# A causal attention pass with its score chunks in reverse, and experts whose transposes stand between two products

## The reference

```
att = jnp.einsum('bthd,bThd->bhtT', q, k) / math.sqrt(HD)
att = jnp.where(causal, -jnp.inf, att)
att = jax.nn.softmax(att, axis=-1)
out = jnp.einsum('bhtT,bThd->bthd', att, v).reshape(Bx, Tx, Cx)
...
dispatched = jnp.einsum('sec,sm->ecm', dispatch, tokens)      # 8 experts, capacity 640 slots
h = jax.nn.relu(jnp.einsum('ecm,emf->ecf', dispatched, w1) + b1[:, None, :])   # 128 -> 512
expert_out = jnp.einsum('ecf,efm->ecm', h, w2) + b2[:, None, :]                # 512 -> 128
combined = jnp.einsum('sec,ecm->sm', combine, expert_out)
```

## Time and profile before

| what | value |
|---|---|
| median of 3 runs | 2424.55 us (2423.39 to 2437.38) |
| profiled execution | 2432.8 us |
| its span | 2430.8 us |
| granted clock of PE over it | 0.844 of full speed |
| causal attention of layer 0 | 178 to 549 us of the span |
| scatter of tokens | 664 to 706 us |
| experts | 716 to 821 us |

### The profile page before, as it was taken

The page is one execution under the profiler, slowest core; times in us unless marked ns, Lnnn a source line. Parts: engine busy times, 40 slices in busy tenths (PEclk is TensorE's granted clock), DMA queues, the critical chain, the costliest instruction groups (busy, mean ns, idle before and its releaser), DMA issues. The chain is left out here.

```text
span 2430.8 us, 43279 instructions
## 1 busy us (share of the span) xinstructions
PE 1873.0 (77%) x12804; PEld 976.6 (40%) x12868; DVE 1448.5 (60%) x2514; ACT 1157.3 (48%) x2802; POOL 892.7 (37%) x999
## 2 busy tenths in 40 slices
PE   5528999884618455629999999557999999999996
PEld 3314444432516334422222222234555555555552
DVE  4426767751401233317888888126888888888882
ACT  1115656560003111104667667305777677677672
POOL 3223344341140332310111111116666677666670
PEclk9768889895559765657999989758999999999997
DMA  3432323322013223232333332130111111111110
GB/s 107 133 101 74 112 92 107 108 84 84 14 63 103 83 85 101 72 94 72 99 108 108 104 105 80 65 111 25 31 48 31 33 43 38 39 52 41 38 49 20
DMA packets 137868, 179.90 MB, mean 74 GB/s; under 512 B 14896, under 2 KB 82355, under 8 KB 137520
## 3 DMA queue, kind: packets, MB, share of 16 engines
q1 hardware_dynamic: 135728, 174.59, 23.3%
q0 software_dynamic: 2048, 4.16, 0.6%
HBM read 97.22 MB, written 66.06 MB: 67 GB/s over the span
## 5 line engine op out<-in xcount | busy, mean ns | idle before, releaser
L910 DVE TENSOR_REDUCE M_sb<-banks 128x1 f32<-128x512 f32 (+3 forms) x1024 | 539.8, 581 | 228.0 <-PE banks L727 124.8
L812 ACT ACTIVATE probs_sb<-banks 128x512 f32<-128x512 f32 (+3 forms) x1024 | 473.5, 520 | 254.9 <-PE banks L753 250.8
L724 PE MATMUL banks<-K_sb,Q_sb 72*128 72x512 bf16 (+3 forms) x1024 | 373.8, 371 | 107.8 <-DMA V_sb<-v_dram 71.5
L753 PE MATMUL banks<-Q_sb,K_sb 75*128 75x512 bf16 (+3 forms) x1024 | 358.6, 357 | 5.9 <-ACT probs_sb L812 3.9
L767 PE MATMUL banks<-probs_sb,V_sb 128*32 128x512 f32 (+3 forms) x2048 | 249.9, 556 | 11.8 <-ACT osum_sb L823 8.6
L724 PEld LDWEIGHTS banks<-K_sb,Q_sb 72*128 72x128 bf16 x1024 | 103.2, 101 | 385.2 <-DVE M_sb L910 225.2
L1773 ACT ACTIVATE l_p_sb<-banks,l_nb_sb,l_inv_sb 128x128 f32<-128x128 f32 x512 | 228.0, 465 | 12.7 <-DVE l_nb_sb L1945 12.5
L1851 POOL TENSOR_TENSOR l_inv_sb<-l_clip_sb,l_minus_half_sb 128x16 f32<-128x16 f32 x64 | 186.2, 2909 | 57.2 <-DVE l_clip_sb L1920 55.3
L1859 POOL TENSOR_TENSOR l_pn_sb<-l_p_sb,l_rs_sb 128x512 f32<-128x512 f32 x128 | 150.1, 1173 | 145.5 <-DVE l_rs_sb L1951 144.0
L1844 POOL TENSOR_TENSOR l_ts_sb<-l_t_sb 128x1024 f32<-128x1024 f32 x64 | 153.4, 2396 | 41.1 <-DVE l_t_sb L1899 24.0
L1579 PE MATMUL banks<-lw_sb,l_xs_sb 128*128 128x512 f32 x256 | 127.8, 623 | 26.4 <-DMA l_xs_sb<-hx 22.8
(11 more groups left out here) (205 smaller groups left out, 3575.1 us busy)
## 6 DMA issues: line engine op xcount, KB each, us to landing
Q_sb<-qk_dram SPq DMA_DIRECT2D x192, 96.0 KB
v_dram<-vpad_sb SPq DMA_DIRECT2D x16, 1024.0 KB, 8.5
V_sb<-v_dram SPq DMA_DIRECT2D x64, 256.0 KB
o_dram<-osum_sb SPq DMA_DIRECT2D x64, 256.0 KB, 5.3
l_vs_sb<-l_vt_sb SPq DMA_DIRECT2D x112, 128.0 KB, 2.3
qk_dram<-parts_sb SPq DMA_DIRECT2D x96, 128.0 KB
K_sb<-qk_dram SPq DMA_DIRECT2D x32, 288.0 KB
x_norm_sb<-x SPq DMA_DIRECT2D x24, 256.0 KB, 2.7
```

The lines of the kernel that those rows point to most:

```text
L724: mm = pe.matmul(out[:, 0:width], g.Q[0:RK, slot, h, k * P:(k + 1) * P], g.K[0:RK, slot, hk(h), 0:width], start=True, stop=not causal)
L753: pe.matmul(SB[ring % 3][:, t0:N], g.K[0:RM, q, hk(h), k * P:(k + 1) * P], g.Q[0:RM, q, h, t0:N], start=True, stop=True).then_inc(s["b_sco ...
L812: act.activation(g.probs[:, k, h, t0:N], SB[ring % 3][:, t0:N], ACT.Exp, scale=scale)\
L910: dve.reduce_max(g.M[:, u % 2, k, h:h + 1], SA[ring % 3][:, 0:width], AX.X, negate=True)\
```

## The change

In the causal layer, `a_tile` and `maxima` go through the query chunks from the last to the first (`query_chunk`), 512 keys first and 128 last. `b_tile`, the exponentials and the products with V keep their order. Where the loop index was compared with 0 it is still the loop index.

In `experts`, the transposes of expert e + 1 (`turn`) stand between the first product (`widen`) and the second (`narrow`) of expert e; `exT` and `eh` get two buffers each, and the answer banks alternate across experts. The wait for the biases at an expert's end is gone from PE; the first uses of the second product wait tile by tile. The loads are split: slots have a semaphore of their own and are loaded once the transposes of the expert two before are done; weights and biases are loaded after that expert's answers are stored. The weights of the first two experts are loaded by SP in the block in which GpSimd scatters. The first and last pair are written out ahead of and behind the loop.

```diff
+    def query_chunk(j):
+        return CH - 1 - j if causal else j
...
-            def a_tile(i, u, k, h):
-                n = u * per + k * UH + h
+            def a_tile(i, u, j, h):
+                n, k = u * per + j * UH + h, query_chunk(j)
...
-            def maxima(i, u, k, h):
-                n = u * per + k * UH + h
+            def maxima(i, u, j, h):
+                n, k = u * per + j * UH + h, query_chunk(j)
...
+        @block.sync
+        def _(sp):
+            for e in range(2):
+                load_weights(g, sp, e, e)
...
-    g.eh = g.sb("eh", [P, F // P, CAP])
-    g.exT = g.sb("exT", [P, CAP])
+    g.eh = g.sb("eh", [P, 2, F // P, CAP])
+    g.exT = g.sb("exT", [P, 2, CAP])
...
+                    e = i * 2 + par
+                    if not last:
+                        sp.wait_ge(s["turned"], e + 1)
+                        load_slots(e + 2, par)
+                    sp.wait_ge(s["biased"], (e + 1) * ST)
+                    sp.dma_start(g.answers_by_expert[e], tile(ys[par])).then_inc(s["stored"], 16)
+                    if not last:
+                        load_weights(g, sp, e + 2, par)
...
+            def turn(e, par, nth):
+                pe.wait_ge(g.eload[par], nth * 16 + 16)
+                pe.wait_ge(s["xT"], e * 2)
+                for t in range(ST):
+                    bank, col = (g.bank[0], t * P) if t < 4 else (g.bank[1], 0)
+                    mm = pe.transpose(bank[:, col:col + P], tile(xs[par])[:, t, :], g.ident[:, :])
+                mm.then_inc(s["turned"], 1)
...
+                    widen(e, par, i)
+                    if not (last and par):
+                        turn(e + 1, par ^ 1, i + par)
+                    narrow(e, par)
...
-                    pe.wait_ge(s["biased"], (i * 2 + par + 1) * ST)
...
+                    if not (last and par):
+                        copy_turned(e + 1, par ^ 1)
                     for t in range(ST):
+                        bias(e, par, t)
```

More of the change, by code:

```diff
@@ L1174, in tile, with pairs @@
         return t.rearrange("p a n -> p (a n)")[:, 0:CAP].rearrange("p (s c) -> p s c", c=C)
+    def pairs(engine, two):
+        two(0, True, False)
+        with engine.Fori(1, E // 2 - 1) as i:
+            two(i, False, False)
+        two(E // 2 - 1, False, True)
     with nc.Block() as block:
@@ L1178, in _, with load_slots, two @@
         def _(sp):
[L1179 to L1184, removed]
+            def load_slots(e, par):
                 sp.dma_start(tile(xs[par]), g.slots_by_expert[e]).then_inc(g.eload[par], 16)
-            def two(i, last):
+            def two(i, first, last):
                 for par in range(2):
[L1189 to L1200, removed]
+                    e = i * 2 + par
[6 more added lines that the diff above has]
+                        load_weights(g, sp, e + 2, par)
+            for e in range(2):
+                load_slots(e, e)
+            pairs(sp, two)
             sp.wait_ge(s["stored"], 16 * E)
@@ new lines, in widen @@
+            def widen(e, par, nth):
+                pe.wait_ge(g.ewload[par], nth * 64 + 64)
+                pe.wait_ge(s["xT"], e * 2 + 2)
+                for f in range(FT):
+                    for half in range(2):
+                        n = f * 2 + half
+                        if not (isinstance(e, int) and e * 8 + n < 4):
+                            pe.wait_ge(s["relu"], e * 8 + n - 3)
+                        pe.matmul(g.bank[2 + n % 4][:, 0:HALF], g.ew1[:, par, f * P:(f + 1) * P],
+                                  g.exT[:, par, half * HALF:(half + 1) * HALF], start=True, stop=True)\
+                          .then_inc(s["hidden"], 1)
@@ new lines, in narrow @@
+            def narrow(e, par):
+                pe.wait_ge(s["relu"], e * 8 + 8)
+                for t in range(ST):
+                    if not (isinstance(e, int) and e * ST + t < 2):
+                        pe.wait_ge(s["biased"], e * ST + t - 1)
+                    bank = g.bank[6 + (par * ST + t) % 2]
+                    for f in range(FT):
+                        mm = pe.matmul(bank[:, 0:C], g.eh[:, par, f, t * P:(t + 1) * P],
+                                       g.ew2[:, par, f * C:(f + 1) * C], start=(f == 0), stop=(f == FT - 1))
+                    mm.then_inc(s["answer"], 1)
@@ new lines, in two, with _ @@
+            def two(i, first, last):
+                for par in range(2):
+                    e = i * 2 + par
+                    widen(e, par, i)
+                    if not (last and par):
+                        turn(e + 1, par ^ 1, i + par)
+                    narrow(e, par)
+            turn(0, 0, 0)
+            pairs(pe, two)
+        @block.scalar
+        def _(act):
+            def two(i, first, last):
+                for par in range(2):
+                    e = i * 2 + par
+                    if not first:
+                        act.wait_ge(s["answer"], (e - 1) * ST)
+                    for f in range(FT):
@@ L1232, in _ @@
[L1232 to L1242 removed]
+                            act.wait_ge(s["hidden"], e * 8 + n + 1)
@@ L1253, in _ @@
                     for t in range(ST):
-                        dve.wait_ge(s["answer"], (i * 2 + par) * ST + t + 1)
-                        dve.tensor_tensor(tile(ys[par])[:, t, :], g.bank[6 + t % 2][:, 0:C], g.eb2[:, par, :],
-                                          ALU.add).then_inc(s["biased"], 1)
+                        bias(e, par, t)
+            copy_turned(0, 0)
+            pairs(dve, two)
 def combine(g, x1, x2):
```

70 lines of the change are left out of this document (28 added, 42 removed).

## The result

The changed kernel took 2402.01 us in the median of 4 runs (2399.23 to 2405.19). The kernel before stood at 2430.97 (4 runs, 2423.39 to 2441.49) with the runs made beside it, so its first three runs had come out low. The ratio is 0.9874, 95% interval 0.9838 to 0.9911: about 29 us, or 1.3%, less.

A forecast was written before the change was run, and what follows sets the result against it. PE was taken as the bound, ending last in both touched stages, so its waits were what could change. -2 - 21.1 - 2.3 = -25.4 us from a median of 2424.55 gave 2400 us, range 2388 to 2413.

The forecast's parts named there:

- sum of 25.4 us: Whole kernel: 2 us less in the causal pass, 21.1 in the experts, 2.3 at the experts' start.
- Steady unit: Causal pass: reversed chunks make a unit 9.29 us against 9.52, in 23 units 5.3 us less.
- mask's chain: Causal pass: chunk 3's product waits for GpSimd's mask, 3.13 us after chunk 2's start; chunks 2 and 3 together 3.70 us.
- Unit with the reciprocals: Causal pass, q = 1 in seven batches, waiting on a DMA: +0.5 us each, +3.5 in all, bounds -3.5 and +7.
- arithmetic of the wait: Causal unit q = 1: first reciprocal starts 4.2 us into the unit against 3.30; 0.9 later, minus 0.7, is +0.2.
- rival (the clock): Causal pass: mask's chain out of the way or clock no longer falling in q = 1; -12 us, so 2389; chance 0.13.
- Experts: Experts' stage: a step takes 9.76 us, seven steps 69.3 with branches against 90.42, so 21.1 us less.
- slow first products: Experts: two of seven first products take 6.26 us instead of 4.57; counted as gone, 3.3 us; if they stay, gain 17.8.
- Start: Start of the experts: slots issued first land 2.0 to 3.0 us earlier; 2.3 us less was taken.
- upper end of 3.0: Start of the experts: if descriptors start in order within one queue, slots wait today for four weight transfers; gain 3.0 us.
- Loads: Experts: moved weight loads take about 5.9 us, PE needs them 9.76 later; slack 3.9 us, nobody waits.
- rule of the Trainium skill: Causal pass: frequent micro-idles of PE make the clock oscillate, so 0.2 us waits in every chunk would cost clock; set aside.

The follow-up runs named there:

- the longer chain: The changed kernel with one more small GpSimd operation of 0.19 us ahead of every mask; chunk 3 took 1.82 us against 1.67, the one run 2403.9 us.

## Why the prediction was right, point by point

- *The time.* 2400 was forecast and 2402.0 measured, and that close a hit is luck. The sum of 25.4 us was 3.6 too small against the 29.0 of the runs made side by side, and the starting point of 2424.55 was 6.4 too low, since the first three runs of the kernel before lay below its later medians; the two misses have opposite signs. By stages, in the profiles: causal pass 2 forecast and 5.2 found, seven steps of the experts 21.1 and 22.5, start 2.3 and 1.2.
- *Steady unit.* The steps were 2.44, 3.15, 2.00, 1.70, the profile has 2.44, 3.11, 2.02, 1.67 or 1.68. The unit gained 0.27, not 0.23; the ones with the output projection gained 0.16 (10.28 to 10.12), and the first of the pass 1.1. In 23 units that is about 6 us. That the mask's chain sets chunk 3 was argued from one row and is shown by the longer chain: +0.15 there and nowhere else.
- *Unit with the reciprocals.* +0.5 was taken; over six units the mean went from 15.08 to 15.11, and with the experts' part alone, in the old order too, it is 15.74: by these the sign is open. The arithmetic of the wait was right (reciprocal 4.3 us into the unit, 4.2 forecast).
- *What was missed.* The step that the next unit would stay as it is. It has the output projection, and in the old order the slow clock sometimes lasts into it. The forecast saw one length of slow stretch, the 6.2 us of the earlier trace rows, while the same trace held a batch of 47.9 us beside five of 44.1 to 44.9 and a last one of 38.8. The reversal alone measured -8.7 by medians, not -2; that is the size at which its rival (the clock) had been put, -12, with a chance of 0.13. But the rival's own account, that the clock no longer falls in q = 1, is not what happened: in the changed kernel's profile it still fell once in each of the seven batches, and only the longest stretches are missing. Shown is that stretches of 17 us occur in the old order (four in two profiles) and not in the new one (none in six), and that nothing of the kind is left where the wait is gone. Why a slow stretch lasts 7 or 17 us is not settled.
- *Experts.* Seven steps: 69.3 forecast, 67.9 measured. The loops' branches cost nothing visible, which is most of the 1.4. That the slow first products would go with the waits was right in every profile that has the change. The reason given was too simple: the first product at 771.97 stands behind the same two waits, 0.97 and 1.07 us, and was not slow. The gain from the place of the transposes was measured by itself: 13.3 us in the profile, 14.2 in the time.
- *Start.* 2.3 forecast, 2.4 in the profile, but the first product was slow throughout (7.45 against 6.23), which took back 1.2: the step that an earlier start is kept in full was wrong. With the weights loaded late PE started 3.1 later. The upper end of 3.0, put down to an order on the queue, had the size right, but 1.8 of the 3.1 is the time to issue four loads, which needs no such order.
- *Loads.* Weights were never waited for. The last of each landed 2.2 to 4.4 us before its first product, where 3.9 was worked out.
- *The rule of the Trainium skill* on short stands between groups of matmuls (TensorE: Matmul & The Clock Gate, "A second HAM failure mode: psum-queue depth-cycling") was set aside since waits of 0.2 us cost no clock. For these it stays so: all steady units run at the upper level. But in the kernels with moved reciprocals the clock fell near stands of 1.05 us and less, so the statement that only the 2.04 us stand costs clock does not carry over; there the traces agree with the rule. They do not say when it bites: the same stands of 0.90 and 0.71 us came in six batches of one profile, and the clock fell in one.

## What to carry to other kernels

A wait costs twice on PE: its own length, and the slow stretch behind it. The second can be the larger: a stand of 2.2 us was followed by 17 us at half the clock with PE busy throughout. So before balancing the work of a loop, look for the one wait in it that is long, and move what waits (here four reciprocals) a step later; that was worth as much as the whole change, and two steps later next to nothing. Read which layers a line serves before you forecast its edit. Two orders of tiles of different width are compared by walking one period, chunk by chunk, and asking at each end which chain arrives last; sums of busy time do not change and tell nothing. If one batch of seven in a trace is 3 us longer than the others, look at it before the forecast: it is a second mode of the loop, and an edit may change how often it comes.

## What the hardware showed that was not expected

- Around one stand of about 2 us PE's granted clock fell and stayed at its lower level for 6.8 us in one batch and for 17.1 us in another, in the same loop with the same work.
- The clock fell between stands of 0.68 and 0.37 us, less than one us apart, while one of 0.72 us (before 306.46 in the kernel before) had no slow matmul behind it, and stands of 0.90 and 0.71 us within 2 us had none in five batches of six.
- Four runs of one kernel lay up to 34 us apart in step with the mean granted clock, 0.855 to 0.837.
- A transfer of 320 KB landed 2.9 to 3.3 us after its issue with nothing in front on its queue and one transfer behind, and 3.7 to 4.5 us with four others in front and five behind.
